# The second bias's sums from split operands in a two-layer LoRA kernel: four single passes of the whole array in place of two full-precision column-tiled products

## The reference

```python
x = x + (x @ W0.T + b0 + 2 * (x @ A0[i0]) @ B0[i0])          # 8 batches x 256 tokens, 1024 -> 1024, rank 16
x = x + (x @ W1.T + b1 + (x @ A1[i1].T) @ B1[i1].T)          # the same tokens, other adapters
```

## Time and profile before

| | |
|---|---|
| median of 3 runs | 284.68 us (284.08 to 284.77) |
| the profiled execution | 284.42 us |
| its span, first to last instruction | 282.8 us |
| TensorE busy | 278.3 us (98%), 1319 matmuls |
| VectorE busy | 215.2 us (76%) |
| ScalarE busy | 102.3 us (36%) |
| GpSimd busy | 19.3 us (7%) |
| DMA | 33.92 MB, 120 GB/s over the span |

### The profile page before, as it was taken

How to read it: one execution, slowest core, us unless ns; L and a number is a source line. 1 busy time by engine, 2 the same in 40 slices (tenths; PEclk the granted TensorE clock), 3 DMA queues, 4 the chain that set the end, 5 groups by cost and what they waited for, 6 DMA issues and landing times.

```text
span 282.8 us, 3853 instructions
## 1 busy us (share of the span) xinstructions
PE 278.3 (98%) x1319; PEld 224.5 (79%) x1319; DVE 215.2 (76%) x318; ACT 102.3 (36%) x141; POOL 19.3 (7%) x45
## 2 busy tenths in 40 slices
PE   7999999999999999999999999999999999999995
PEld 5888888888868887877888878888878888878885
DVE  5789999999899899967975873865873875865413
ACT  4565464262965574322331231141221131321100
POOL 3333200400000001000000100000000000000000
PEclk9999999999999999999999999999999999999999
DMA  6997000100365400451622802712701712212002
GB/s 217 391 409 309 31 1 2 57 19 0 129 230 211 139 14 19 158 185 76 206 74 76 261 37 75 236 46 80 249 37 74 239 43 93 75 39 86 25 37 111
DMA packets 13095, 33.92 MB, mean 120 GB/s; under 512 B 2149, under 2 KB 2405, under 8 KB 13078
## 3 DMA queue, kind: packets, MB, share of 16 engines
q1 hardware_dynamic: 11906, 31.60, 31.6%
q0 software_dynamic: 1024, 2.10, 2.3%
q10 hardware_dynamic: 148, 0.00, 0.0%
HBM read 22.09 MB, written 11.60 MB: 119 GB/s over the span
## 4 chain that ended last, share of the span: by engine, by line
PE 98%; DVE 0%; issue 0%
PE bank L1227 18%; PE bank L1228 18%; PE bank L1229 18%; PE bank L1065 9%; PE bank L1069 9%; PE bank L1070 9%; PE bank L1258 3%; PE bank L1234 3%; PE bank L1083 1%; PE bank L1105 1%; PE bank L1097 1%; PE bank L1099 1%; PE bank L1098 1%; PE bank L1085 1%; PE bank L1084 1%; PE bank L1167 1%
## 5 line engine op out<-in xcount | busy, mean ns | idle before, releaser
L1227 PE MATMUL bank<-ops,late 128*128 128x512 f32 x192 | 75.5, 393 | 0.0
L1228 PE MATMUL bank<-ops,late 128*128 128x512 f32 x192 | 74.9, 390 | 0.0
L1229 PE MATMUL bank<-ops,late 128*128 128x512 f32 x192 | 74.8, 389 | 0.0
L1069 PE MATMUL bank<-ops 128*128 128x512 f32 x112 | 43.8, 391 | 0.0
L1070 PE MATMUL bank<-ops 128*128 128x512 f32 x112 | 43.6, 390 | 0.0
L1227 PEld LDWEIGHTS bank<-ops,late 128*128 128x128 f32 x192 | 36.1, 188 | 9.5 <-issue 2.1
L1229 PEld LDWEIGHTS bank<-ops,late 128*128 128x128 f32 x192 | 36.1, 188 | 7.7
L1228 PEld LDWEIGHTS bank<-ops,late 128*128 128x128 f32 x192 | 36.1, 188 | 7.4
L1065 PE MATMUL bank<-ops 128*128 128x512 f32 x112 | 41.1, 401 | 0.0
L484 ACT CAST late<-rows 128x512 fp32r<-128x512 f32 x24 | 14.7, 622 | 52.3 <-DVE rows L762 26.0
L484 ACT CAST late<-raw_a 128x512 fp32r<-128x512 f32 x24 | 14.8, 624 | 30.6 <-PE bank L1234 21.1
(11 more groups left out here) (153 smaller groups left out, 379.4 us busy)
## 6 DMA issues: line engine op xcount, KB each, us to landing
raw_a<-xT SPq DMA_DIRECT2D x16, 512.0 KB, 4.8
out<-raw_a SPq DMA_DIRECT2D x27, 256.0 KB, 2.0
a<-rb_rows SPq DMA_DIRECT2D x8, 392.0 KB
raw_a<-W1T SPq DMA_DIRECT2D x2, 1024.0 KB, 12.6
raw_b<-W SPq DMA_DIRECT2D x2, 1024.0 KB, 16.3
rb_rows<-b_hl SPq DMA_DIRECT2D x3, 512.0 KB
rb_rows<-late SPq DMA_DIRECT2D x3, 512.0 KB
raw_a<-U SPq DMA_DIRECT2D x4, 256.0 KB, 4.4
```

The source lines that it names most:

```text
L1069: mm(bank[:, :], left(u, 0, k, m), op_k(v, 1, k), start=False, stop=False, skip_group_check=on_top)
L1227: mm(bank[:, :], hi, t_op(t, 0, k), start=(start and k == 0), stop=False, skip_group_check=not start)
L1228: mm(bank[:, :], hi, t_op(t, 1, k), start=False, stop=False, skip_group_check=not start)
L1229: last = mm(bank[:, :], lo, t_op(t, 0, k), start=False, stop=(k == KH - 1), skip_group_check=not start)
```

## The change

`ones_b` becomes 128 x 160 of type fp32r: zeros, with ones in columns 32 to 63 (two memsets on GpSimd with a semaphore ones_made). A window of 128 columns from column 32 on has its ones in the first 32 output rows, a window from column 0 has them in the next 32. ScalarE casts bias_sum into b1_hl's high part, VectorE subtracts for the low part, and TensorE makes four passes of the full array (2 halves x high and low), all adding into one bank. Since b1_hl is used again, ScalarE's cast waits for b1_bounced and r_summed in place of VectorE's `combine("t2", ...)`, which now waits for c_summed. The subtraction that gives the low part of the factor differences (a_diff_lo) moves up on VectorE, from after `low("us1")` to after `combine("vt4", ...)`.

```diff
--- before.py
+++ after.py
@@ -68,7 +68,7 @@
             return ctx.enter_context(nc.semaphore(name))
 
         idx = sb("idx", [1, 2 * B], I32)
-        ones_b = sb("ones_b", [P, P], F32)
+        ones_b = sb("ones_b", [P, P + CT], F32R)
         b0_raw = sb("b0_raw", [P, KT], F32)
         b0_sum = sb("b0_sum", [P, KH], F32)
         ops = sb("ops", [P, 6, 2, QUAD], F32R)
@@ -119,6 +119,9 @@
         b_sums = c_rows[:, :].rearrange("p (k n) -> p k n", k=KH)
         a_diff_raw, b_sum_raw = factor_sums[:, 0, :], factor_sums[:, 1, :]
 
+
+        bias_hl = b1_hl
+        ones_at = [ones_b[:, CT:CT + P], ones_b[:, 0:P]]
         CW = HALF
         c_hl = [c_rows[0:NH * CT, part * CW:(part + 1) * CW] for part in range(2)]
 
@@ -192,6 +195,7 @@
         last_stored = [sem(f"last_stored{n}") for n in range(2)]
         ident_made = sem("ident_made")
         masks_made = sem("masks_made")
+        ones_made = sem("ones_made")
         bias_zeroed = sem("bias_zeroed")
         diag_added = sem("diag_added")
         diag_v22 = sem("diag_v22")
@@ -374,7 +378,9 @@
             pool.wait_ge(ident_made, 1)
             nc.gpsimd.affine_select(out=ident[:, :], in_=ident[:, :], compare_op=ALU.not_equal, fill=1.0, base=0,
                                     pattern=[[-1, P]], channel_multiplier=1).then_inc(ident_made, 1)
-            nc.gpsimd.memset(ones_b[:, :], 1.0)
+            nc.gpsimd.memset(ones_b[:, :].bitcast(F32), 0.0).then_inc(ones_made, 1)
+            pool.wait_ge(ones_made, 1)
+            nc.gpsimd.memset(ones_b[:, CT:2 * CT].bitcast(F32), 1.0).then_inc(ones_made, 1)
             nc.gpsimd.memset(same_batch[:, :, :], 1.0).then_inc(masks_made, 1)
 
             pool.wait_ge(masks_made, 1)
@@ -567,6 +573,11 @@
             for m in ORDER_M6[2:]:
                 act.wait_ge(r_lo, m + 1)
                 put_e1(m)
+
+            act.wait_ge(r_summed, NH)
+            act.wait_ge(b1_bounced, 3 * DMA)
+            act.wait_ge(bias_step, 2 * KT)
+            nc.scalar.copy(bias_hl[:, 0, :], bias_sum).then_inc(b1_split, 1)
             high("vt1")
             act.wait_ge(summed["us1"], 1)
             high("us1")
@@ -949,25 +960,26 @@
             dve.wait_ge(lo[SLOT["v21"]], filled("v21", 2))
             dve.wait_ge(bias_step, 2 * KT)
             combine("vt4", "v21", "vt2", ALU.subtract)
+            dve.wait_ge(a_diff_hi, 1)
+            nc.vector.tensor_tensor(a1[:, KH:KT, BR:2 * BR].rearrange("p k (b r) -> p b k r", b=B),
+                                    a_diff_raw.rearrange("p (b k r) -> p b k r", b=B, k=KH),
+                                    a1[:, KH:KT, 0:BR].rearrange("p k (b r) -> p b k r", b=B), ALU.subtract
+                                    ).then_inc(a_diff_lo, 1)
             low_r(0)
             low_r(1)
             dve.wait_ge(summed["us3"], 1)
             combine("us1", "u21", "u22", ALU.add)
             low("u22")
+            dve.wait_ge(b1_split, 3)
+            nc.vector.tensor_tensor(bias_hl[:, 1, :], bias_sum, bias_hl[:, 0, :], ALU.subtract).then_inc(b1_split, 1)
             low("us1")
-            dve.wait_ge(a_diff_hi, 1)
-            nc.vector.tensor_tensor(a1[:, KH:KT, BR:2 * BR].rearrange("p k (b r) -> p b k r", b=B),
-                                    a_diff_raw.rearrange("p (b k r) -> p b k r", b=B, k=KH),
-                                    a1[:, KH:KT, 0:BR].rearrange("p k (b r) -> p b k r", b=B), ALU.subtract
-                                    ).then_inc(a_diff_lo, 1)
             low("vt1")
             low("vt4")
 
             dve.wait_ge(t3_kept, KH)
             dve.wait_ge(d11_kept, KH)
 
-            dve.wait_ge(r_summed, NH)
-            dve.wait_ge(b1_bounced, 3 * DMA)
+            dve.wait_ge(c_summed, 1)
             combine("t2", "d11", "t3", ALU.add)
             dve.wait_ge(c_split, 1)
             nc.vector.tensor_tensor(c_hl[1], b_banks[2][0:NH * CT, :], c_hl[0], ALU.subtract).then_inc(c_split, 1)
@@ -1192,10 +1204,12 @@
                 row_block("us2", "vt2", a_banks[m], m, True).then_inc(m_done[6], 1)
 
             pe.wait_ge(t3_kept, KH)
-            pe.wait_ge(bias_step, 2 * KT)
+            pe.wait_ge(b1_split, 4)
+            pe.wait_ge(ones_made, 2)
             for j in range(NH):
-                last = mm(b_banks[2][j * CT:(j + 1) * CT, :], ones_b[:, 0:CT], bias_sum[:, j * CW:(j + 1) * CW],
-                          start=True, stop=True)
+                for part in range(2):
+                    last = mm(b_banks[2][:, :], ones_at[j], bias_hl[:, part, j * CW:(j + 1) * CW],
+                              start=(j == 0 and part == 0), stop=(j == NH - 1 and part == 1))
             last.then_inc(c_summed, 1)
 
             pe.wait_ge(lo[SLOT["us1"]], filled("us1", 1))
```

## The result

The changed kernel takes 294.9 us (median of 6 runs, 293.65 to 295.83) against 284.47 us of before (6 runs, 284.07 to 284.94). The ratio is 1.0372, with a 95% interval from 1.0353 to 1.0391: slower by 10.4 us. The forecast was 296.2 us with a range of 293.0 to 298.0. The profiled execution took 295.58 us, with a span of 294.0 us against 282.8.

What follows compares the result with a forecast made beforehand. TensorE, 98% of the chain, was taken to bound the kernel. The sum was 284.68 us, the median of before, plus 8.9 us of waiting and 2.6 us of clock: 296.2 us, range 293.0 to 298.0.

Steps and rivals of the forecast that it cites:

- Step 1: TensorE's bias sums: four single passes take 0.91 us instead of 1.18, -0.27 us if TensorE arrives free.
- Step 2: ScalarE's cast into b1_hl waits for b1_bounced, free at 73.3, released at 84.5; three casts queue behind it for 11 us.
- the landing: DMA bounce out of b1_hl: taken to land just before 84.50, from a 0.2 us hold of VectorE's L674.
- +8.9: TensorE's factor product L1083 begins at 91.5 instead of 82.63, waiting for us1's rest: 8.9 us lost.
- Rival B: Bounce lands earlier, at 79.6, something else held L674: 288.7, up to 291.3 us with the clock; chance 0.08.
- C: Rival: no stall, b1_bounced in by 75.5, only the matmuls' gain of 0.27 us: 284.4 us; chance 0.03.
- Step 4: TensorE's waits: 5.2 us for b1_split, then us1's rest at 91.47, 6.97 us after the landing; 8.9 us lost.
- Step 5: VectorE's earlier split of the factor differences, 0.68 us moved into 0.80 us of idle: costs nothing, gains nothing.
- Step 8: Later work: helpers shifted 9.3 us, next tight place the first rank product; given back or added: zero, at most 0.5 us.
- Step 9: Clock: TensorE idles 5.2 and 3.8 us, falls to half rate, product begins at that rate: +2.6 us.
- Rival A: The clock holds through TensorE's hole: 293.6 to 293.9 us; chance 0.14.

Runs made afterwards that it cites:

- own_place: Changed kernel with the split bias sums in late's fourth part, cast waiting for ScalarE's puts instead of b1_bounced: 284.42 us, ratio 1.0008.
- wait_only: Kernel before with one added wait, ScalarE for b1_bounced ahead of its cast of vt1: 295.6 us, ratio 1.0402.
- fill: Changed kernel with 20 spare TensorE passes ahead of the bias sums and 14 behind them: 293.07 us, ratio 1.0314.
- adiff_only: Kernel before with only the subtraction for the factor differences moved to its earlier place: 284.52 us, ratio 1.0008.
- ones_only: Kernel before with only the 160-column ones_b, its two memsets and the wait between them, ones used as float32: 284.61 us, ratio 1.001.
- bounce_first: Changed kernel with SyncE's three DMAs of b1_hl issued ahead of the t_sums wait and turn: 289.67 us, ratio 1.0193.
- sums_behind: Changed kernel with the bias's cast and subtraction behind those of vt1, us1 and vt4, and the four passes behind the factor product: 286.53 us, ratio 1.0077.

## Why the prediction was right

- **The bound.** That TensorE was the path and had 3.3 us to spare against us1's rest was right (against the factor differences, over at 79.26 + 0.68 = 79.94, it was 2.7). own_place put 2.1 us of new work (0.96 and 1.13 to the next start) into that slack without a wait.
- **Step 1, the passes.** 0.94 us instead of 1.18 in own_place, forecast 0.91. In the changed kernel it is lost in the hole, as said.
- **Step 2 and the landing.** The mechanism was right: the changed kernel names the DMA that holds the cast, which idles 10.36 us and starts at 85.03, 2.7 us behind the last pass of m6; I had 84.50, 3.2 behind it. That is the 0.5 us between my +8.9 and the measured +8.42. Rival B (79.6) and C (75.5) are out, and the landing is 13.9 us behind the start of the issue, 9.9 behind its end. The fixed cost of about 2 us that the Trainium skill gives in DMA: Bandwidth & Descriptors is a small part of that.
- **How the landing was dated.** Here luck had a part. The gap of 0.2 us before L674 has no releaser in the view, and that this DMA made it is not shown. The releases of the changed kernel, wait_only and fill come 13.6 to 13.9 us behind the start of the issue; counted from 70.25 that is 83.9 to 84.2, just ahead of 84.28 (84.35 - 0.07), where L674 could have started anyway. In adiff_only the same instruction starts 13.8 us behind the issue without a gap, in ones_only 14.3 behind it without one. What the row does give is that the landing was in by 84.50. The forecast took that bound as the landing; it lay close to it because VectorE happened to be free just then.
- **Step 4, the chain of 6.97 us.** Measured 7.03 in three kernels: the changed one, bounce_first and fill (91.28 - 84.25).
- **Step 5.** Nothing in the sum, and nothing in adiff_only. But "gains nothing" holds only while TensorE does not wait for VectorE: wait_only shows 0.6 us that the early place saved inside the hole. The forecast had it in by taking us1's rest as last.
- **Step 8.** m5 to the rank product takes 22.34 us against 22.35: zero, as taken. (3 x 2.2 from 89.2 is 95.8, not 95.9; nothing hangs on it.) The place named there as next tight is the one that opened in sums_behind.
- **Step 9, the clock.** Right in kind, too large: 2.6 us forecast, 1.75 in the bill, 1.65 by fill. The start of the kernel had 13 passes at half rate; behind the second hole it was 8. The clock had been down since the first hole, through the four passes with ones. By the stretches shown above it had fallen at about 85.6, while TensorE idled, and was granted in full again at about 95.8. How many passes it catches differs between profiles (8 here, 12 in wait_only and bounce_first), and by the mean clock also between runs of one kernel. In bounce_first the run with a mean clock of 0.988 took 290.66 us and those with 0.993 to 0.994 took 289.24 to 289.85. Rival A (the clock holds) is out: the mean clock was 0.982 to 0.987 in all six runs. The trace agrees with what the prediction took from the Trainium skill (TensorE: Matmul & The Clock Gate, the section on HAM oscillation): TensorE left idle came back at half rate.
- **Sum.** 296.2 forecast, 294.9 measured: 0.9 of the difference is the clock and 0.5 the landing. What the bill leaves of the measured shift (10.43 - 10.17 = 0.26) works the other way and is about offset by the lower median of before, 284.47 instead of 284.68.

## What to carry to other kernels

Before a dead-looking buffer is used again, ask who still reads it, DMAs above all, and when the last of them lands; a buffer whose last reader stands earlier in the same engine's stream, as in own_place, cost no wait. A wait is priced by what is queued behind it on its engine: the same landing cost at most 0.2 us on VectorE before, 8.4 of TensorE's time in front of ScalarE's casts, 5.9 behind them (7.17 - 1.30), and none at the sums where TensorE had other work, though there t2 behind the sums held the rank product for 1.57. A single wait without a named releaser gives a time by which a DMA had landed, which no row of the profile gave; it does not show that the DMA was what was waited for.

## What the runs showed of the hardware

- 1.57 MB from SBUF to DRAM in three transfers took 12.7 to 13.9 us from the start of the issue to the release, with loads and stores of the same queue behind it; issued 3.6 us earlier in the kernel's work (bounce_first), they landed 4.7 us earlier.
- TensorE's granted clock went from 2.4 to 1.2 GHz in a hole of 4.7 us and stayed down through four passes, a second hole and the next passes of the stream, 8 in the profile of the changed kernel and 12 in that of wait_only. In bounce_first it fell in a hole of 3.45 us. 34 spare passes in the holes of the changed kernel kept it up, and the kernel with them was 1.65 us faster.
- The sums of 128 partitions in two halves of 512 columns took TensorE 1.18 us as two float32 products in column tiles and 0.94 us as four fp32r passes of the whole array (own_place).
